# Graph network stack, 1 core: one split ahead of each first quarter of a pass among T steps; normalisation pieces behind the quarters

## What is computed

```
x = layernorm(x + layer(x, adj))          # over the 64 features
layer 0: As = [I, A, 2 A A - I];  out[n] = sum_k (As[k] x)[n] @ w[n, k];  w[n] = sum_d embedding[n, d] weight[d]   (d = 16)
layer 1: z = relu(A z w_i), twice
layer 2: x @ w_self + (A x) @ w_neighbor + bias
layer 3: [x, A x, 2 A A x - x, A x, 2 A A x - x] @ weight + bias
```

## Time and profile before

| | us |
|---|---|
| median of 3 runs | 1267.96 (1266.08 to 1274.63) |
| the profiled execution's own time | 1270.8 |
| its span, first to last instruction | 1268.7 |
| mean granted TensorE clock | 0.991 of full |

### The profile page before, as it was taken

How to read it: one execution, slowest core, us unless ns; L and a number is a source line. 1 busy time by engine, 2 the same in 40 slices (tenths; PEclk the granted TensorE clock), 3 DMA queues, 4 the chain that set the end, 5 groups by cost and what they waited for, 6 DMA issues and landing times.

```text
span 1268.7 us, 16356 instructions
## 1 busy us (share of the span) xinstructions
PE 1232.3 (97%) x5872; PEld 1030.6 (81%) x5872; DVE 758.6 (60%) x1863; ACT 215.5 (17%) x392; POOL 62.0 (5%) x52
## 2 busy tenths in 40 slices
PE   7999999999999999999999999997999999999996
PEld 6888888788878887878888888886888888888875
DVE  5826897787777777788725654542146355544624
ACT  6622111121112101110111111100111111110110
POOL 0000000000000000000000001010000000010100
PEclk9999999999999999999999999998999999999998
DMA  9732112211111111110011143033001110330320
GB/s 346 318 100 59 38 49 64 71 50 42 46 51 62 39 38 38 30 50 13 15 34 34 30 88 67 1 98 85 1 18 50 34 34 25 84 67 9 92 59 35
DMA packets 127783, 78.16 MB, mean 62 GB/s; under 512 B 97217, under 2 KB 107969, under 8 KB 125633
## 3 DMA queue, kind: packets, MB, share of 16 engines
q1 hardware_dynamic: 127696, 77.04, 20.6%
HBM read 53.42 MB, written 23.59 MB: 61 GB/s over the span
## 4 chain that ended last, share of the span: by engine, by line
PE 86%; DVE 6%; DMA 3%; SPq 2%; issue 1%; ACT 1%; DVEq 0%; ACTq 0%
PE ps L652 27%; PE ps L653 27%; PE ps L756 20%; PE ps L670 7%; PE ps L691 2%; PE ps L692 2%; SPq L1129 2%; DVE nat L1018 1%; DVE ring L1018 1%; DMA td<-ring 1%; DMA raw<-in_at 1%; PE ps L664 1%; DVE xs L916 1%; DMA td<-stg 1%; DMA nat<-zd 1%
## 5 line engine op out<-in xcount | busy, mean ns | idle before, releaser
L652 PE MATMUL ps<-B,xs 128*128 128x512 f32 x1664 | 657.1, 395 | 12.2 <-DVE xs L916 12.2
L653 PE MATMUL ps<-B,xs 128*128 128x512 f32 x1664 | 650.4, 391 | 0.0
L652 PEld LDWEIGHTS ps<-B,xs 128*128 128x128 f32 x1664 | 313.6, 188 | 76.7 <-issue 10.0
L653 PEld LDWEIGHTS ps<-B,xs 128*128 128x128 f32 x1664 | 313.9, 189 | 62.4
L756 PE MATMUL ps<-Tw,xs 128*128 128x512 f32 x1280 | 309.4, 391 | 2.5 <-DVE ring L1018 2.5
L756 PEld LDWEIGHTS ps<-Tw,xs 128*128 128x128 f32 x1280 | 238.6, 188 | 55.0 <-DVE ring L1018 4.8
L904 DVE TENSOR_TENSOR ring<-ps,rrep 128x512 f32<-128x512 f32 x94 | 64.5, 689 | 245.9 <-PE ps L653 236.0
L1018 DVE SCALAR_TENSOR_TENSOR nat<-ps,embn,nat 128x128 f32<-128x128 f32 x448 | 154.0, 344 | 51.0 <-PE ps L756 50.7
L1018 DVE SCALAR_TENSOR_TENSOR ring<-ps,embn,ring 128x128 f32<-128x128 f32 x512 | 175.5, 343 | 0.0
L670 PEld LDWEIGHTS ps<-W,ring 128*128 128x128 f32 x896 | 111.6, 191 | 10.6 <-DVE ring L904 3.7
L670 PE MATMUL ps<-W,ring 128*128 128x128 f32 x896 | 113.3, 275 | 2.8 <-DVE ring L904 2.4
(11 more groups left out here) (66 smaller groups left out, 547.6 us busy)
## 6 DMA issues: line engine op xcount, KB each, us to landing
raw<-in_at SPq DMA_DIRECT2D x13, 1024.0 KB, 16.1
td<-ring SPq DMA_DIRECT2D x32, 256.0 KB, 2.1
ring<-td SPq DMA_DIRECT2D x128, 64.0 KB, 2.5
ring<-in_xn SPq DMA_DIRECT2D x16, 256.0 KB, 2.8
ring_x<-in_xt SPq DMA_DIRECT2D x32, 128.0 KB, 3.2
ring_x<-y1d SPq DMA_DIRECT2D x32, 128.0 KB, 3.3
out<-nat SPq DMA_DIRECT2D x16, 256.0 KB, 2.8
y1d<-ring SPq DMA_DIRECT2D x14, 256.0 KB, 2.7
```

The costliest lines, as they stand in the source:

```text
L652: pe.matmul(bank, x[:, 0, m, :], of, start=m == 0, stop=False)
L653: mm = pe.matmul(bank, x[:, 1, m, :], of, start=False, stop=ends and m == NT - 1)
```

## The change

Four things in the list of steps, and one name in DVE's part:

1. For passes (2,1), (3,1) and (2,3) (`ahead`), `split_ahead` goes. Split 0 comes right behind the last scale of the pass before; splits 1, 2 and 3 each come right ahead of the quarter that reads them, so behind the T step that the weave puts between two quarters.
2. `join`, `centre`, `deviate`, `normed` of a chunk within a weave come behind the quarters that follow the T step, not ahead of them. In `closing`, split 3 of passes (2,0) and (3,0) comes ahead of `deviate`.
3. Weaves 1 and 2 have one piece less to place (29 for 30), and weave 3 begins its quarters one T step later (lead 3 for 2).
4. DVE's sums for layers 2 and 3 move from the `W` step to a new step `sums` ahead of pass (2,4). `reload` of pair 2 comes behind split 3 of pass (2,3).

```diff
+    def ahead(j, p):
+        return p == 1 and j > 1 or (j, p) == (2, 3)
...
+            if ahead(j, p) and c == 0 and 0 < m:
+                put("split", j, p, m)
+                if m == 3 and j == 2 and p == 3:
+                    put("reload", j)
             put("mm", j, p, c, m)
...
+        if ahead(j, p + 1):
+            put("split", j, p + 1, 0)
         put("after", j, p, 3)
...
         if i == 2:
-            put("deviate", j, 1, 3)
             if j < 2:
                 put("split", j + 2, 0, 3)
+            put("deviate", j, 1, 3)
...
-                if c > 0 and half == 0:
-                    put(("join", "centre", "deviate", "normed")[e], j, min(e, 1), c - 1)
...
                 yield
+                if c > 0 and half == 0:
+                    put(("join", "centre", "deviate", "normed")[e], j, min(e, 1), c - 1)
...
-    def split_ahead(j, p):
-
-        for c in range(NC):
-            put("split", j, p, c)
-            if c % 2:
-                yield None
...
-        yield from split_ahead(j, 1)
+        yield None
         yield from one_pass(j, 1)
...
+            if (j, p) == (2, 4):
+                put("sums")
             splits(j, p)
...
-    weave(1, products, 30, 2, 2, coming)
+    weave(1, products, 29, 2, 2, coming)
...
-    weave(2, products, 30, 2, 2, coming)
+    weave(2, products, 29, 2, 2, coming)
...
-    weave(3, products, 22, 2, 0, None)
+    weave(3, products, 22, 3, 0, None)
...
-                    if s.kind == "W":
+                    if s.kind == "sums":
                         dv.wait_ge(s_w, 48)
```

More of the change, by code:

```diff
@@ L221, in layer1 @@
         yield from one_pass(j, 2)
-        yield from split_ahead(j, 3)
-        if j == 2:
-            put("reload", j)
+        yield None
         yield from one_pass(j, 3)
```

## The result

The changed kernel takes 1312.06 us (median of 6 runs, 1306.39 to 1314.56) against 1268.36 before: a ratio of 1.033, 95% interval 1.031 to 1.035. It is 44 us slower. The forecast was 1306, range 1289 to 1321. The profiled execution took 1314.6 us, which makes it the slowest of the six. Their times go with the mean granted TensorE clock: 1306.39 us at 0.984, 1311.19 at 0.981, 1314.56 at 0.978.

A forecast was written before the change was run, and what follows sets the result against it. PE was taken as the bound, busy 97% of the span. Waits of +28.1 us on the profiled 1270.8, less 2.8 for the median, made 1296; clock falls of +10 made 1306 us, range 1289 to 1321.

The forecast's parts named there:

- The mechanism: Passes (2,1), (3,1), (2,3): PE waits at quarters for splits queued behind T-step accumulations; net +11.6, +11.6 and +8.6 us.
- The sum of the waits: Whole kernel: all waits and gains together +28.1 us, giving 1296 us without clock falls; that case had chance 0.32.
- The clock: Weaves: PE's clock falls to half after about four of nine long waits, 2.6 us each, +10 us; chance 0.50.
- The 23 us: Weaves: rival that the clock falls at all nine long waits, 23 us more than 1296, so 1319; chance 0.08.
- The length of the stand: Weaves: new waits of 3.2 to 4.6 us exceed the stands of 3.3 and 2.1 us before known clock falls.
- Split 3 ahead of deviate: Passes (2,0) and (3,0): the cast no longer queues behind the square root; gain 1.0 us twice, -2.0.
- Lead 3: Weave 3: a quarter's wait gives 1.45 us back, the fourth T step costs 0.8; -0.6 taken.
- Sums: Layer sums moved far behind the weights' DMA: PE's 0.95 us wait for a scale goes, -1.1 us.
- The pieces: `join` and normalisation pieces moved by one quarter: taken as nothing, within +-1 us in all.
- Not slower: Heads of the passes: rival that each quarter finds its split done and present losses go, 1260 us; chance 0.05.
- Half the waits: Weaves: rival that waits are half as long because DVE's accumulations overlap PE's T step, 1282 us; chance 0.05.

The follow-up runs named there:

- e1: Changed kernel with splits 1 to 3 of passes (2,1), (3,1), (2,3) each put ahead of the T step before their quarter; 1265.51 us, ratio 0.9985.
- e4: Changed kernel with 12 to 18 extra PE matmuls, results unread, filling each of the nine long waits; 1297.47 us, ratio 1.024.
- e6: e2 with lead 2 instead of 3 in weave 3, as in the kernel before; one execution, 1267.02 us.
- e8: e2 with the normalisation pieces ahead of the quarters again, split 3's place in closing kept; one execution, 1265.08 us.
- e3: Kernel before with part 1 alone (splits right ahead of their quarters), plus its 29 pieces and place of reload; 1322.86 us, ratio 1.043.
- e5: Changed kernel with splits 1 to 3 single, each at least one T step ahead of its quarter, quarter 0 behind two T steps; 1261.77 us, ratio 0.9935.
- e7: e1 with split 1 alone put back behind its T step, as in the changed kernel; 1281.67 us, ratio 1.0085.
- e2: Changed kernel with part 1 undone: splits two and two ahead of two T steps, as before; 1262.61 us, ratio 0.9961.

## Why the prediction was right, and where it was short

- *The mechanism* was read from the order alone and held: a split behind a T step, with the quarter right behind both, waits for a whole set of accumulations. Forecast shown idle 2.9 to 4.4 us at nine places and 1.8 at two, about 31 us; measured 2.94, 3.55, 2.94 twice, 4.50, 2.94, 3.55, and about 1.77 twice: 33.4 in all. e1 shows it by moving only these splits.
- *The sum of the waits* was 1296; e4, which has the waits and not the clock, gives 1297.5.
- *The clock* is the term that was mis-sized. I took four falls of 2.6 us, +10; e4 puts the cost at 14.6. What came out too small is "a fall at about four of the nine long waits": the trace of the changed kernel has a fall at eight of them. The price of one was nearly right: PE worked 4.5 us in such a stretch on average, which costs 2.3 us for the 2.6 taken. So the profiled execution lost some 18 us, and the other runs, most of them shorter and at a higher clock, probably less. That 1306 lies within 6 us of 1312 owes something to this term being small beside the waits; the range allowed it 0 to 20 us. The Trainium skill's rule (TensorE: Matmul & The Clock Gate, "HAM oscillation — how this bites in real kernels"), each wait a fall, was nearer in the number of falls than I was. The 23 us that I put beside it were too high, since they took 2.6 us for each of nine.
- *The length of the stand* did not separate the cases as I had it. I wrote that the new waits of 3.2 to 4.6 us were longer than the two stands before falls, but one of those is 3.3 us by the same rows. In the runs the same 2.94 us shown idle had a fall behind it at most places and none at 454.61, with the clock at 1.00 from 452 to 462; and two of the eight falls came only after PE had started again, 1.2 us after 284.58 and 0.6 after 445.72. Which waits get one stays open.
- *Split 3 ahead of deviate*: the wait of 0.77 at the earlier trace rows is gone; the split now starts at 228.77, and PE does not stop:

```profile
228.77 0.68 DVE L919 TENSOR_TENSOR xs<-ring_g,xs 128x512 fp32r<-128x512 f32 x1
229.37 0.68 DVE L963 TENSOR_REDUCE sml<-ring 128x8 f32<-128x512 f32 x1
230.09 0.30 ACT L829 ACTIVATE sml<-sml,epst 128x8 f32<-128x8 f32 x1 [2.12 <-DVE sml L963]
```

- *Lead 3*: forecast -0.6, and e6 shows 0.6 with the new wait at the fourth T step, where it was forecast. *Sums*: the wait of 0.95 us at the earlier trace rows is gone, PE's `after` there (L673) starts without idle time:

```profile
661.32 1.05 PE L673 MATMUL ps<-W,ring 128*128 128x128 f32 x8
```

- *The pieces*, which I put at nothing outside pass (2,3), were right as a move by itself (e8) and wrong as a cover: with the pieces ahead of the quarters, quarter 3 of passes (2,1) and (3,1) waits 2.9 us longer each, 5.8 of the 11 us that e3 lies above the changed kernel.
- *Rivals.* "Not slower" fell with the first wait; but what it asked for, a split that ends before PE gets to its quarter, is what e1 and e5 make, and e5's 1261.8 is near the 1260 that the rival priced. "Half the waits" fell too: the nine waits have their full length.

## What to carry to other kernels

Where engines walk one list of steps, ask of each helper step (here a split) not how near it stands to its use but what its own engine has queued ahead of it, and whether that needs the engine which will wait. A helper put just in time behind a step that both engines share turns their overlap into taking turns; here one such step earlier took back 46 us. And in this kernel waits of 3 to 4.5 us on TensorE cost half as much again by the clock (15 us on 29), so price the clock too.

## What was not expected of the hardware

- Filling nine waits with useless matmuls made the kernel 14.6 us faster (e4), with the clock at 1.00 in the stretches shown where it had been 0.78 to 0.90.
- The same wait of 2.9 us was followed by a fall once and not the other time in one execution (e7), and in the changed kernel eight of nine were.
- The old wait for the reload after the weaves, which no edit here touches, was 8.0 us before, 7.1 in the changed kernel, and from 5.3 (e2) to 8.3 (e4) in the experiments. It moves single profiled spans by up to 3 us, so small effects were read from their place in the trace, not from the span.
